# Graph attention on Trainium2: in head 3 VectorE compares four mask tiles instead of six, ScalarE makes twelve instead of ten

## What is computed

```
seq    = (x @ W_seq).reshape(2048, 16, 32)
score1 = einsum('nhd,d->hn', seq, a1);  score2 = einsum('nhd,d->hn', seq, a2)
scores = leaky_relu(score1[:, :, None] + score2[:, None, :], 0.2)
scores = scores + (1.0 - adj)[None] * -65500.0
attn   = softmax(scores, axis=-1)
hidden = einsum('hij,jhd->ihd', attn, seq).reshape(2048, 512)
out    = layernorm(x + elu(hidden @ W_out + b_out))
```

## Time and profile before

| | us |
|---|---|
| time, median of 3 runs | 519.34 (519.14 to 520.39) |
| the profiled execution: time | 520.75 |
| the profiled execution: span, first to last instruction | 519.0 |
| mean granted TensorE clock, share of full speed | 0.996 |

### The profile page before, as it was taken

How to read it: one execution, slowest core, us unless ns; L and a number is a source line. 1 busy time by engine, 2 the same in 40 slices (tenths; PEclk the granted TensorE clock), 3 DMA queues, 4 the chain that set the end, 5 groups by cost and what they waited for, 6 DMA issues and landing times.

```text
span 519.0 us, 15251 instructions
## 1 busy us (share of the span) xinstructions
PE 501.0 (97%) x6744; PEld 454.4 (88%) x6744; DVE 460.2 (89%) x577; ACT 433.0 (83%) x462; POOL 34.8 (7%) x64
## 2 busy tenths in 40 slices
PE   8999999999999989999999999999999999899993
PEld 7888888999999989999999999999999999644542
DVE  3457679998999999999999999999998879988886
ACT  2776779798999889999999999999995989266664
POOL 3000000000000010000000000000000000035444
PEclk9999999999999999999999999999999999999998
DMA  7999993402020301202021020202202040025443
GB/s 249 414 313 343 342 304 72 164 3 82 3 83 2 124 30 55 83 3 83 3 83 56 30 83 3 83 1 83 80 7 82 3 144 3 1 68 155 125 142 120
DMA packets 30721, 53.28 MB, mean 103 GB/s; under 512 B 18496, under 2 KB 19776, under 8 KB 26688
## 3 DMA queue, kind: packets, MB, share of 16 engines
q1 hardware_dynamic: 30104, 51.79, 30.2%
q10 hardware_dynamic: 552, 0.52, 0.3%
HBM read 43.78 MB, written 4.33 MB: 93 GB/s over the span
## 4 chain that ended last, share of the span: by engine, by line
PE 73%; DVE 13%; ACT 6%; issue 4%; DMA 3%; POOL 0%; ACTq 0%; DVEq 0%; POOLq 0%; SPq 0%
PE sums L475 35%; PE bank L489 18%; PE sums L568 10%; PE sums L400 6%; DVE tring L816 4%; ACT tring L614 3%; DVE tring L811 3%; DMA Vp<-in_adj_dram 1%; PE bank L556 1%; PE sums L387 1%; DVE Vp L866 1%; DMA Vp<-in_L_gnn_W_seq_dram 1%; DVE Vp L792 1%; ACT Vp L631 1%; DVE xp L860 1%
## 5 line engine op out<-in xcount | busy, mean ns | idle before, releaser
L614 ACT ACTIVATE tring<-abc,ab 128x2048 int8<-128x2048 f32 x150 | 292.4, 2023 | 2.7 <-DMA abc<-a_rows 2.7
L475 PE MATMUL sums<-Vp,tring 128*128 128x132 f16 x4096 | 241.6, 221 | 3.6 <-DVE tring L816 1.9
L475 PEld LDWEIGHTS sums<-Vp,tring 128*128 128x128 fp8e4 x4096 | 236.9, 98 | 5.6 <-issue 3.5
L816 DVE TENSOR_TENSOR tring<-adj,tring 128x1024 uint32<-128x1024 uint32 (+1 forms) x134 | 155.9, 1174 | 11.7 <-ACT tring L614 7.5
L489 PE MATMUL bank<-Vp,adj 128*128 128x132 f16 x2048 | 126.1, 221 | 3.3 <-DVE Vp L866 3.3
L489 PEld LDWEIGHTS bank<-Vp,adj 128*128 128x128 fp8e4 x2048 | 122.1, 96 | 3.7 <-DVE Vp L866 3.6
L811 DVE TENSOR_SCALAR tring<-abc,ab 128x2048 int8<-128x2048 f32 x90 | 115.5, 1284 | 0.0
L568 PE MATMUL sums<-abc,Vp 128*128 128x512 f32 (+1 forms) x136 | 57.5, 568 | 0.1
L568 PEld LDWEIGHTS sums<-abc,Vp 128*128 128x128 f32 x136 | 24.7, 190 | 22.7 <-issue 22.0
L652 ACT ACTIVATE low<-sums 128x33 f32<-128x33 f32 (+3 forms) x66 | 20.1, 393 | 22.3 <-PE sums L475 22.3
L592 ACT ACTIVATE tring<-Vp 128x2048 int8<-128x2048 f32 x16 | 30.6, 1914 | 5.9 <-DMA Vp<-in_adj_dram 5.9
(11 more groups left out here) (116 smaller groups left out, 370.3 us busy)
## 6 DMA issues: line engine op xcount, KB each, us to landing
Vp<-in_adj_dram SPq DMA_DIRECT2D x16, 1024.0 KB, 8.4
abc<-a_rows SPq DMA_DIRECT2D x15, 1024.0 KB, 4.8
abc<-in_x_dram SPq DMA_DIRECT2D x16, 256.0 KB, 7.3
Vp<-in_x_dram SPq DMA_DIRECT2D x16, 256.0 KB, 3.0
out_dram<-Vp SPq DMA_DIRECT2D x16, 256.0 KB, 2.2
abc<-in_L_gnn_W_out_dram SPq DMA_DIRECT2D x1, 1024.0 KB, 5.3
Vp<-in_L_gnn_W_seq_dram ACTq DMA_DIRECT2D x2, 256.0 KB, 5.4
Vp<-in_L_gnn_W_seq_dram SPq DMA_DIRECT2D x2, 256.0 KB, 6.1
```

Source lines behind the costliest of these rows:

```text
L475: mm = pe.matmul(bank[b][:, c * 2 * VW:(c + 1) * 2 * VW], slot(jt)[:, it * P:(it + 1) * P].bitcast(F8), Vp[:, h, jt, :, :], start=(jt == 0 ...
L614: return act.activation(slot(jt)[:, columns], row(h)[:, columns], ACT.Sign, bias=ab[:, jt, H + h:H + h + 1], scale=-1.0)
L816: return dve.tensor_tensor(words, edges, words, ALU.bitwise_and)
```

## The change

The table gives head 3 the tiles 4, 5, 10, 11 for VectorE, where it had 2, 3, 6, 7, 12, 13. All other heads keep theirs.

```diff
 FOUR, SIX, EIGHT = (4, 5, 10, 11), (2, 3, 6, 7, 12, 13), (2, 3, 6, 7, 10, 11, 14, 15)
-DVE_TILES = ((4, 5, 6, 7, 10, 11, 14, 15),) + (SIX,) * (H - 4) + (EIGHT, SIX, FOUR)
+DVE_TILES = ((4, 5, 6, 7, 10, 11, 14, 15),) + (SIX, SIX, FOUR) + (SIX,) * (H - 7) + (EIGHT, SIX, FOUR)
```

## The result

| | us |
|---|---|
| kernel before, 9 runs on the same chip | 519.69 (518.99 to 521.12) |
| changed kernel, 9 runs | 522.87 (521.24 to 524.30) |
| ratio | 1.0050, 95% interval 1.0036 to 1.0065 |
| profiled execution: span, mean granted clock | 522.1, 0.989 (before: 519.0, 0.996) |

The change makes the kernel slower by 0.5%, 2.6 us by the ratio (1.9 to 3.4). The forecast was slower by 2.2 us. The median lies 0.07 us above the upper end of the range; the kernel before also ran 0.35 us above the median that the sum started from. By the ratio the shift of 2.6 us lies above the sum's 2.20, which is inside the interval.

A forecast was written before the change was run, and what follows sets the result against it. VectorE was taken to bound heads 3 and 4, with TensorE slackless behind 184.44 us. ScalarE's 3.24 us lateness less 1.04 of room gives 2.20 us, so 519.34 + 2.20 = 521.5 us; main case 520.8 to 522.4, stated range 520.0 to 522.8.

The forecast's parts named there:

- the sum: Head 4's first join moves from 168.50 to 170.70, 2.20 us later; added to the median 519.34 this gives 521.5 us.
- What bounds the kernel: VectorE is full in heads 3 and 4; from 184.44 us TensorE has no slack, so any shift there moves the end.
- ScalarE's two masks: Two added masks in head 3, 3.78 us, partly filling idle time: head 4's second mask ends 3.24 us later.
- room: At head 4's join of tiles 0 and 1, ScalarE's second mask was ready 1.04 us ahead of VectorE.
- the filled wait: ScalarE's 0.40 us wait before copy_low at 147.21 is filled by a second mask, so copy_low starts 1.35 us later.
- VectorE's steps in head 3: VectorE's operations timed one by one: line 879 ends at 152.65 instead of 151.78; joins wait for ScalarE.
- Taken alone it would put split_low(7) 2.4 us earlier, and TensorE's 2.17 us would go: Two compares fewer on VectorE, 1.20 us each, save 2.40 us and remove TensorE's stall in the middle of head 4.
- the faster rival: ScalarE's lateness is hidden and VectorE's relief counts: the head 4 stall goes, 517.2 us; chance 8%.
- The clock: Rival: two TensorE stalls drop the clock to 1.2 GHz for head 4's eight tiles, 7.5 us more, 529.0 us; chance 3%.
- The rule: Relieve the engine of highest occupancy first: move work from VectorE to ScalarE in this place, giving 517.2 us.

The follow-up runs named there:

- run 2: Kernel before, with ScalarE making two of its ten head 3 masks twice and VectorE keeping six compares: ratio 1.0047, 58.59 us to the middle of head 4.
- run 5: Changed kernel, but VectorE's four tiles in head 3 are 2, 3, 12, 13: ratio 1.0058 to the kernel before, 58.78 us to the middle of head 4.
- run 6: Changed kernel, but VectorE keeps five compares in head 3 and ScalarE makes eleven masks: ratio 1.0006 to the kernel before, 56.39 us to the middle of head 4.
- run 1: Changed kernel, with two of ScalarE's twelve head 3 masks writing only 64 of 2048 columns: ratio 0.9994 to the kernel before, 55.73 us to the middle of head 4.
- run 7: Kernel before, with VectorE's four reductions for the largest values one step earlier (heads 1 and 2): ratio 0.9986, 55.42 us to the middle of head 4.
- run 4: Kernel before, with split_low(7) moved earlier in head 4 (jt 6 instead of 9): ratio 0.9981, 54.03 us to the middle of head 4.
- run 3: Changed kernel, with 28 useless matmuls in TensorE's wait in the middle of head 4: ratio 1.0046 to the kernel before, 58.25 us to the middle of head 4.
- run 11: The changed kernel measured once more, on the chip of the filled-wait kernels: ratio 1.0055 to the kernel before, 58.30 us to the middle of head 4.
- run 9: Kernel before, with 28 useless matmuls in TensorE's wait in the middle of head 4: ratio 0.9992, 56.01 us to the middle of head 4.

## Why the prediction was right

- **What bounds the kernel** held: VectorE before head 5, and behind 184.44 no slack for a lateness that comes through VectorE. 2.26 us in the middle of head 4 came out as 2.17 us in the time at the full clock. A lateness of TensorE alone does find a little: of the 1.58 us of the low stretch 1.17 reached head 5.
- **ScalarE's two masks** held, 3.24 us less 1.04 of room. Runs 2, 5 and 6 bear out each term: the masks alone (2.58), the filled wait (2.77 without, 2.26 with), one mask (0.38 for 0.31).
- **VectorE's steps in head 3** held within some 0.1 us: waits of 0.82, 1.53, 0.49 and 1.53 us for 0.9, 1.6, 0.6 and 1.6.
- **"Taken alone it would put split_low(7) 2.4 us earlier, and TensorE's 2.17 us would go"** was wrong, and with it the time of 517.2 us of the faster rival. With ScalarE's two extra masks nearly empty run 1 gained 0.28 us, and a relief with no mask moved gained 0.59 in run 7: VectorE can be at most 1.04 us earlier at head 4's first join as long as ScalarE is no earlier, since ScalarE's mask isn't there before. The same number that made the loss caps the gain. What a relief of VectorE gained in the middle of head 4 did reach head 5 (71.09 us in run 1 and 70.78 in run 7, against 71.37); the 1.98 us of run 4, where the load is the same and only the order is another, was asked back there but for 0.18.
- **The clock** was a rival at 3% and 7.5 us. Both were off: the low stretch took 5.54 - 3.96 = 1.58 us, and the like of it was in many executions, of both kernels. Reading one profile of before, whose clock was full behind a stall of 2.17 us, I took that as what such a stall does. It is the likely source of the difference between 2.2 us and the measured 2.6 (by the ratio) to 3.2 (by the medians), as executions at the full clock differ by 2.17. That it is the source isn't shown: run 3 raised the clock and was hardly faster. So the sum got the mechanism, and what lies above 2.2 us it did not foresee.
- **The rule** that the prediction took from the Trainium skill, Perfetto Trace Analysis, "Identifying the Most-Contended Engine", is to optimize the engine of the highest occupancy first. Read as "take work off it", it misleads here: VectorE was the busier engine (24.77 us of 25.05 in head 4), work was taken from it, and the kernel got slower by 0.5%.

## What to carry to other kernels

When work moves between two engines that feed a common join, don't ask which is busier; find the next join behind the move and read how long the other engine's input had been ready there. That distance, 1.04 us here, is both the room for what is moved and, while the other engine stays as it is, the most that the relief can bring, and idle time that the moved work fills counts before it. Look also whether the receiving engine's idle time lies ahead of that join or behind it: ScalarE's 1.95 us lay behind, and did nothing for it.

## What the runs showed of the hardware

A wait of TensorE of about 2 us between dense products was followed in some executions by a stretch of half clock (the 1.2 GHz level), and not in others of the same kernel: the changed kernel's first profiled execution took 5.54 us for the 64 products behind its 2.17 us, the one of run 11 took 3.96 behind the same wait, and had its low stretch behind the wait of 1.91 us instead. The profiled executions of the kernel before and of run 2 kept 1.00 behind 2.17 us, that of run 6 didn't (5.54 us behind 2.18). Low stretches also stood near the start of the kernel (in the profiled executions of the changed kernel and of run 9), and every profiled execution ends at 0.50 (the kernel before from 515.1 us on, behind its last matmuls), so the mean clock of an execution alone doesn't say where it lost. The Trainium skill, TensorE: Matmul & The Clock Gate, "Why this matters for your kernels", warns that idle gaps between bursts, longer ones than these, bring the half clock back. These traces go further than the page: gaps of about 2 us did it too, though in one execution and not in another. Of the groups in the table, the step from the first to the second goes with about 1.2 us in the kernel before (519.35 to 520.56). That is what one low stretch in head 4 cost by the time head 5 began in the changed kernel's profile (1.17 us).
